# Rows of shifts loaded eight tiles behind, padding stored later, and y of three more tiles written by VectorE

## The reference

```python
p = softmax(h @ Wr + br); probs, idx = top_k(p, 2); probs /= probs.sum(-1)
h1 = layernorm(relu(h @ W1[e] + b1[e]), g1[e], be1[e])     # 512 hidden
y  = layernorm(relu(h1 @ W2[e] + b2[e]), g2[e], be2[e])    # 128
out = x + gb * sum over the two experts of prob * y
```

## Time and profile before

| what | value |
|---|---|
| median of 3 runs | 499.58 us (499.39 to 500.2) |
| the profiled execution | 501.55 us, its span 499.8 us |
| busy, share of the span | PE 96%, DVE 90%, ACT 81%, POOL 70% |
| granted clock of TensorE | 0.998 of full speed |
| q1, SP's queue | 71860 packets, 60.48 MB, 48.6% of 16 engines |

### The profile page before, as it was taken

One profiled execution on the slowest core, in us unless ns is written; L12 is line 12 of the kernel. 1 busy time (PEld: TensorE's weight loads), 2 busy tenths in 40 slices (PEclk: granted clock), 3 DMA queues, 4 the chain that ended last, 5 costly groups with the idle time before them and its releaser, 6 DMA issues. The chain is left out here.

```text
span 499.8 us, 15142 instructions
## 1 busy us (share of the span) xinstructions
PE 480.2 (96%) x3151; PEld 373.4 (75%) x3151; DVE 447.7 (90%) x2210; ACT 406.4 (81%) x1118; POOL 349.4 (70%) x461
## 2 busy tenths in 40 slices
PE   7999999999998899999999999999999999999994
PEld 6456666565676788888878888888788888888861
DVE  6878999989897999899998999999899999999994
ACT  3678899988856778787876898989889888989883
POOL 1003676766777777888888778888786888888871
PEclk9999999999999999999999999999999999999999
DMA  6990511124111889877539787577577667567655
GB/s 164 312 260 23 132 51 49 55 70 102 54 49 57 186 168 162 205 233 200 134 93 178 196 199 200 136 207 205 160 192 191 173 184 213 159 177 209 191 176 168
DMA packets 80365, 78.37 MB, mean 157 GB/s; under 512 B 11434, under 2 KB 73053, under 8 KB 80277
## 3 DMA queue, kind: packets, MB, share of 16 engines
q1 hardware_dynamic: 71860, 60.48, 48.6%
q0 software_dynamic: 8416, 16.93, 9.6%
HBM read 55.20 MB, written 22.62 MB: 156 GB/s over the span
## 5 line engine op out<-in xcount | busy, mean ns | idle before, releaser
L703 POOL DMA_INDIRECT expert_rows<-rows_ring,slot x128 | 123.9, 968 | 87.2 <-issue 68.5
L731 POOL DMA_INDIRECT expert_results<-y,target x119 | 120.5, 1012 | 33.2 <-issue 28.8
L1685 PE MATMUL bank<-W,h2T 128*128 x720 | 97.0, 278 | 2.1 <-issue 0.9
L1685 PEld LDWEIGHTS bank<-W,h2T 128*128 128x128 f32 x720 | 87.5, 191 | 14.0 <-issue 7.5
L948 ACT ACTIVATE v<-wmod 128x128 f32<-128x128 f32 x135 | 41.7, 309 | 31.8 <-DVE vg L1463 28.5
L1667 PE MATMUL bank<-W1hi,h3hi 128*128 x135 | 65.4, 485 | 1.5 <-DVE h3lo L1224 1.5
L1229 DVE BATCH_NORM_STATS2 stf<-h1T 128x6 f32<-128x512 f32 x90 | 59.3, 660 | 0.0
L813 ACT ACTIVATE n<-X,nm,rs 128x128 f32<-128x128 f32 x128 | 52.6, 488 | 7.2 <-DVE nm L1392 7.1
L1452 DVE SCALAR_TENSOR_TENSOR wmod<-bank,rse,shifts 128x128 f32<-128x128 f32 x119 | 40.9, 344 | 15.9 <-PE bank L1685 14.4
L960 ACT ACTIVATE sde<-mve,eps 128x2 f32<-128x2 f32 (+1 forms) x138 | 40.7, 295 | 17.8 <-DVE mve L1476 15.6
L1675 PE MATMUL bank<-ident_wr,h1T 128*128 128x128 f32 x360 | 54.5, 274 | 0.1
(11 more groups left out here) (260 smaller groups left out, 1187.0 us busy)
## 6 DMA issues: line engine op xcount, KB each, us to landing
shifts<-expert_shifts SPq DMA_DIRECT2D x119, 192.0 KB
hrow<-expert_rows SPq DMA_DIRECT2D x135, 65.0 KB
xi<-expert_results SPq DMA_DIRECT2D x12, 512.0 KB, 5.5
out_x<-X SPq DMA_DIRECT2D x15, 256.0 KB
X<-in_L_attn_x SPq DMA_DIRECT2D x7, 512.0 KB, 7.4
b_ring<-b_two_parts SPq DMA_DIRECT2D x135, 4.0 KB
W1lo<-in_L_ffn_W SPq DMA_DIRECT2D x4, 512.0 KB, 6.2
expert_rows<-rows_ring,slot POOLq DMA_INDIRECT x128
```

The source lines that it names most:

```text
L703: nc.gpsimd.indirect_dma_start(out=rows_d, out_offset=bass.IndirectOffsetOnAxis(ap=slot[q][:, n // TOPK, n % TOPK:n % TOPK + 1], axis=0), ...
L731: nc.gpsimd.indirect_dma_start(out=results_d, out_offset=bass.IndirectOffsetOnAxis(ap=target[i % TARGETS][:], axis=0), in_=y[k], in_offset ...
L1685: ins = mm(acc, rT[i % DEPTH][:, ch * P:(ch + 1) * P], W2[:, bass.ds(e * CF + ch, 1), :], start=(ch == 0), stop=(ch == CF - 1))
```

## The change

In SP's list the shifts of tiles up to 25 are loaded as before, six tiles behind the rows. At i = 32 and 33 none are loaded, and from i = 34 on the shifts of tile i-8 go with the rows of tile i. After the loop come those of tiles 127 and 128, ahead of the wait for the early sums, and those of 129 to 134 where they were. Padding is stored behind i = 38, 42, ... 66. Tiles 127, 128 and 129 become direct, so that the last eight are. POOL keeps its loop and the order of its stores.

```diff
-        LAST_SHIFTED = EXPERT_TILES - 5
+        LAST_SHIFTED, LAST_GROUPED = EXPERT_TILES - 8, EXPERT_TILES - 5
-            SHIFT_LAG = SLOTS - 2
+            SHIFT_LAG, LATE_SHIFT_LAG, LATE_FROM = SLOTS - 2, SLOTS, 32
                 load_rows(i, i % SLOTS)
-                load_shifts(i - SHIFT_LAG)
+                if i < LATE_FROM:
+                    load_shifts(i - SHIFT_LAG)
+                elif i >= LATE_FROM + LATE_SHIFT_LAG - SHIFT_LAG:
+                    load_shifts(i - LATE_SHIFT_LAG)
-            PADDED_AT = ROUND1 - E
             for i in range(SLOTS, ROUND1):
                 load_next(i)
-                if i >= PADDED_AT:
-                    store_padding(i - PADDED_AT)
+            PADDED_AT = {ROUND1 + 14 + 4 * e: e for e in range(E)}
+            assert max(PADDED_AT) < LAST_ROWS
                 load_next(i)
+                if i in PADDED_AT:
+                    store_padding(PADDED_AT[i])
                 if i in GB_AT:
+            for n in range(EXPERT_TILES - LATE_SHIFT_LAG, EXPERT_TILES - SHIFT_LAG):
+                load_shifts(n)
             sp.wait_ge(early_sum_ready, (EARLY - 1) * J)
-            for i in range(LAST_SHIFTED):
+            for i in range(LAST_GROUPED):
-            for i in range(LAST_SHIFTED - 1, EXPERT_TILES):
+            for i in range(LAST_GROUPED - 1, EXPERT_TILES):
```

## The result

The changed kernel takes **501.23 us**, the median of 20 runs (499.67 to 504.0), against 499.64 us for the kernel before (20 runs, 498.84 to 502.09): a ratio of 1.0033, 95% interval 1.0023 to 1.0044. The forecast was 499.8 us. The range, 497.8 to 501.7, holds the time, but the forecast's case, no change within 0.2%, didn't come: the change is slower by more than that. The traced execution took 502.01 us, its span 499.9, against 501.55 and 499.8 before. So **the two traces differ by 0.1 us of span and the medians by 1.6 us**; that gap is taken up in the part on why the prediction was right or wrong.

The account below looks back on a forecast made before the run. PE, with hardly a gap in the second stage, was taken as the bound, so only what makes it late costs time. +1.5 - 1.04 + 0 - 0.2 = +0.26 us on 499.58 gave 499.8 us, range 497.8 to 501.7.

Parts of the forecast that it names:

- the forecast's case: Whole kernel: no change that a measurement can tell, within about 0.2%, 1.0 us; chance 0.42 together with the third rival.
- Part 1, first place: Lag of eight, tiles 44 to 48: rows stall goes, shifts of 47 and 48 wait behind the 512 KB load; +1.5 us.
- Part 1, second place: Lag of eight at tile 83, group of tiles 80 to 83: its wait for rows goes; -1.04 us.
- Part 2: Padding moved from tiles 16 to 23 to between 38 and 66: 0 us, bounds -0.3 and +0.5.
- Part 3: y of tiles 127 to 129 at the end: POOL's last store 1.56 us sooner, VectorE's values 0.88 later; -0.2 us.
- a difference between two kernels carries over: Last step: rows from an execution of 501.55 us, 2 us above the median; +0.26 added to the median 499.58.
- The sum: Whole kernel: +1.5 - 1.04 + 0 - 0.2 = +0.26 us.
- The slower one: Rival: tile 38's results land in 5.73 us, tile 48's values +3.6, sum +2.3, 501.9 us; chance 0.28.
- It does not do what it says: Rival: rows are late for a cause of their own and nothing moves, 499.6 us; chance 0.05.
- The faster one: Rival: first 512 KB load goes at once, both landings at 2.61 us; -1.6 us, 497.9; chance 0.30.

Follow-up runs that it names:

- e7: Kernel before with the lag of eight and the first 512 KB load behind i = 56, not 54; padding and tail as before: 497.62 us, ratio 0.9958.
- e9: Kernel before with the lag of eight, padding moved and first 512 KB load behind i = 56; tail as before: 500.03 us, ratio 1.0008.
- e6: The changed kernel once more, unchanged, for a second profiled execution: 501.04 us, ratio 1.0032 to the kernel before.
- e3: Kernel before with only y of the last eight tiles changed as in the change (tiles 127 to 129 by VectorE): 500.04 us, ratio 0.9991.
- e4: The changed kernel with the first 512 KB load two places later, behind i = 56 and not 54: 499.96 us, ratio 1.0001 to the kernel before.
- e10: Kernel before with the lag of eight, the new tail and first 512 KB load behind i = 56; padding as before: 498.11 us, ratio 0.9963.
- e12: e4 with all eight padding counts read into SP's registers at i = 38: 500.35 us, ratio 0.9995 to the kernel before.
- e5: The kernel before once more, unchanged, for a second profiled execution: 499.47 us, ratio 0.9999.
- e1: Kernel before with the lag of eight alone, padding and last y as before: 501.16 us, ratio 1.0024.
- e11: Kernel before with only the first 512 KB load moved, behind i = 56: 500.3 us, ratio 1.002.

## Why the prediction was right in its steps and wrong for the median

- **Part 1, first place: right to 0.3 us in every instant.** The landing was taken as 3.6 us and took 3.60. Predicted and measured: the load 272.4 and 272.13, tile 47's shifts 273.6 and 273.53, tile 48's 277.3 and 277.06, tile 48's values 280.8 and 280.59, VectorE's waits 2 to 4 us and 3.68. By the start of tile 54 the changed kernel is 1.16 us behind (283.05 against 281.89), where the step had +1.5. Two details failed: of the old stall 0.32 us were to stay, and none did; and the wait for tile 44's own shifts, 0.72 us, wasn't foreseen. The shifts took 3.73 and 3.53 us from issue to use (the step had 3.46). That fit is partly luck: over all the traces such waits show 3.15 to 5.95 us. The rule that the prediction took from the Trainium skill ("DMA: Bandwidth & Descriptors", Anatomy of one DMA), 2.45 us by its figures, is too short here; it is stated for GpSimd's path, and SP issues these loads.
- **Part 1, second place: right.** -1.04 predicted, -1.03 measured (1.28 us behind at tile 83, 0.25 at tile 84).
- **Part 2: right for this kernel, by its cover.** The wait for tile 38's results covers what the padding takes. But the price behind that cover was given as one issue of 0.35 us; the gap of 1.8 us in front of the fifth padding, there in the kernel before at 189.85, was left out. e7 and e9 show that the padding costs 0.5% once the cover is gone.
- **Part 3: right inside the span.** Values come 0.81 us later against tile 134's start (0.88 predicted: from 481.08 - 471.11 = 9.97 against 479.77 - 470.61 = 9.16), POOL's last store 1.96 sooner (1.56 predicted), the tail -0.38 (-0.2 predicted). Of the three new operations one took 0.49 us and not 0.35, begun 0.13 us behind POOL's add at 474.86; by the Trainium skill's rule ("SBUF — State Buffer", SBUF: two separate sides) it could have lost what was left of that operation, 0.33 us; it lost 0.14. **Outside the span the tail gives it all back**: in the 80 executions of the kernels that have it (after and e6, e3, e4, e10, e12) device time is 2.11 to 2.22 us longer than the span, in the 72 of the seven other runs 1.75 to 1.85. The step had no term for this 0.36 us. Its cause isn't in the trace, and is open.
- **The step that failed is the last: "a difference between two kernels carries over".** The sum, +0.26, was right for traced executions: +0.1 of span in the first pair, -0.1 in the second (499.1 in e6, 499.2 in e5). The medians say +1.6. Of this 0.36 lies outside the span. The rest, some 1.2 us, is the place of the traces among the executions: before's two traced executions are among its slowest (501.55 and 500.96 against medians of 499.64 and 499.47), after's are nearer to theirs (502.01 and 501.3 against 501.23 and 501.04). So it was the choice of one slow execution as the base that failed. The traces don't show where its time went. The working subtracted from 279.28, tile 48's values in that execution; in e5 and e3, with the same code up to there, they are at 278.18 and 278.69. But both then wait for rows (PE 0.94 us at 284.71 and 1.22 at 285.44) and start tile 56 at 287.27 and 287.97, no sooner than before's first trace (286.78), against 288.06 in the changed kernel. The old place has a second stall that comes when the first is short, and the missing 1.2 us isn't there. Which of before's stalls is shorter in its median execution can't be seen in these runs; that part is open.
- **The rivals.** The slower one has the sign and the place, but not its price: it wanted a landing of 4.3 us and more, and it was 3.60. That the range holds the time is therefore luck in part: its upper end stood for that landing, and what came there was 0.36 us outside the span and 1.2 from the choice of the base. "It does not do what it says" falls: both stalls for rows went. The faster one needed a landing of 2.61 us. Shifts that don't stand behind the held load, made by hand in e7, are the version that wins.

## What to carry to other kernels

A load that is moved back in an in-order queue must be followed past everything in that queue that waits, reads registers or issues for long: here the lag paid 0.42% once the held 512 KB load was moved with it (e7), and cost 0.24% without that (e1). A stall that ends when another engine gets on has no length of its own: it can soak up earlier lateness, and it wanders (tile 49 at 268.96 to 270.03), so its worth has to be read from several executions and not from one. A price that the trace of the kernel before already shows, as the 1.8 us gap in front of the fifth padding, moves with the operation even if it cost nothing where it stood. And a gain under 1 us in a trace is no gain until the time outside the span has been looked at.

## What was not expected of the hardware

- PE's granted clock fell behind waits of 1.48 us (0.79 and 0.78 over 4 us, after) and 1.91 (0.77, e6), but neither behind 1.69 in e11, 1.41 in e9, nor 0.97 and 0.95 in e1. At 160 to 164 us PE is busy 2.13 to 2.17 of 4 us in all fourteen traces, and a fall followed in five of them (0.62 to 0.71 over 164 to 168 us, 1.00 in the others).
- Where SP reads four counts into its registers, 1.75 to 1.85 us pass without an issue or a wait (the fifth padding, thirteen traces), five times an issue.
- From issue to use, the shifts (192 KB) took 3.15 to 5.95 us in the fourteen waits behind 240 us that the profile puts down to them: 3.27, 3.53 and 5.30 in the changed kernel, 3.15 in e4, 5.95 in e9. The 512 KB loads have a median of 5.1 us from issue to landing.
- Three more y in one operation of VectorE, and fewer on POOL and ScalarE, lengthen the time outside the span by 0.36 us (medians 2.16 and 1.80); the two groups, of 80 and 72 executions, don't overlap. e3, which changes nothing else, has it too (2.12 to 2.21).
